# A two-layer transformer on one core: the image loads ahead of the weights, a bias folded into weights, powers apart, and a new stage order with three added matmuls

## The reference

```python
h = _L0_tok_ref(x, L0_tok_channel_weights)
h = jnp.concatenate([h, txt], axis=1)
h = h + _L0_attn_ref(_layernorm(h, axis=-1), ...)
h = h + _L0_ffn_ref(_layernorm(h, axis=-1), ...)
h = h + _L1_attn_ref(_layernorm(h, axis=-1), ...)
h = h + _L1_ffn_ref(_layernorm(h, axis=-1), ...)
```

## Time and profile before

| | us |
|---|---|
| median of 3 runs | 4835.94 (4804.51, 4835.94, 4847.9) |
| the profiled execution, whole | 4793.07 |
| its span, first to last instruction | 4791.3 |
| TensorE busy | 4135.2 (86% of the span) |
| VectorE, ScalarE, POOL busy | 2621.2, 1759.9, 402.3 |
| mean granted TensorE clock | 0.855 of 2.4 GHz |

### The profile page before, as it was taken

One profiled execution on the slowest core, in us unless ns is written; L12 is line 12 of the kernel. 1 busy time (PEld: TensorE's weight loads), 2 busy tenths in 40 slices (PEclk: granted clock), 3 DMA queues, 4 the chain that ended last, 5 costly groups with the idle time before them and its releaser, 6 DMA issues.

```text
span 4791.3 us, 70127 instructions
## 1 busy us (share of the span) xinstructions
PE 4135.2 (86%) x27744; PEld 3228.1 (67%) x27744; DVE 2621.2 (55%) x7217; ACT 1759.9 (37%) x2774; POOL 402.3 (8%) x523
## 2 busy tenths in 40 slices
PE   2779888889888989888889888989889888989888
PEld 1556677676676767677676667767667776766666
DVE  2455555555655555555555655555655555565433
ACT  1234333334333334333334333344433333433332
POOL 2100000000000000000000000000000000000000
PEclk8678888888889888888888888888888888888888
DMA  4111111101111101111101111101111110111000
GB/s 113 31 27 34 32 26 36 33 21 34 32 26 36 33 21 34 32 26 36 33 21 34 32 29 34 36 17 34 36 32 26 36 33 21 34 26 16 13 13 4
DMA packets 154046, 147.13 MB, mean 31 GB/s; under 512 B 64359, under 2 KB 132026, under 8 KB 153722
## 3 DMA queue, kind: packets, MB, share of 16 engines
q1 hardware_dynamic: 153722, 142.64, 14.0%
HBM read 87.28 MB, written 7.91 MB: 20 GB/s over the span
## 4 chain that ended last, share of the span: by engine, by line
PE 62%; DVE 19%; SPq 5%; ACT 5%; DMA 4%; issue 3%; POOL 3%; POOLq 0%; DVEq 0%; ACTq 0%
PE area_a L1034 13%; PE area_n L1042 11%; PE area_b L1034 8%; PE area_m L1042 7%; SPq L457 5%; PE area_n L1259 4%; DMA k1s<-scratch 3%; PE area_n L1066 3%; DVE mx L938 3%; PE area_m L1209 2%; ACT pT_both L666 2%; PE area_a L1117 2%; PE area_b L1057 2%; DVE scratch L949 1%; PE area_m L1066 1%
## 5 line engine op out<-in xcount | busy, mean ns | idle before, releaser
L938 DVE TENSOR_REDUCE mx<-area_n 91x1 f32<-91x273 f32 x1152 | 472.1, 432 | 246.5 <-PE area_n L1259 236.1
L1042 PE MATMUL area_n<-w_dn,hid 128*91 128x192 f32 x2304 | 494.8, 380 | 46.5 <-DVE mrow L943 38.7
L1034 PE MATMUL area_a<-xT,w_gu 96*128 96x273 f32 x1536 | 446.4, 438 | 61.7 <-DVE y L898 38.2
L1042 PEld LDWEIGHTS area_n<-w_dn,hid 128*91 128x91 f32 x2304 | 426.4, 190 | 95.3 <-issue 60.3
L1259 PE MATMUL area_n<-k1s,q1s 96*91 96x273 bf16 x1152 | 350.1, 359 | 152.5 <-DVE mx L938 92.9
L1034 PE MATMUL area_b<-xT,w_gu 96*128 96x273 f32 x1536 | 430.3, 426 | 0.0
L1034 PEld LDWEIGHTS area_a<-xT,w_gu 96*128 96x128 f32 x1536 | 305.0, 208 | 154.2 <-DVE y L898 48.0
L1259 PEld LDWEIGHTS area_n<-k1s,q1s 96*91 96x91 bf16 x1152 | 142.3, 141 | 335.3 <-DVE mx L938 227.2
L1034 PEld LDWEIGHTS area_b<-xT,w_gu 96*128 96x128 f32 x1536 | 313.0, 208 | 73.1
L611 ACT ACTIVATE pa<-area_a,scal 91x820 bf16<-91x820 f32 x192 | 180.3, 939 | 302.3 <-PE area_a L1117 278.2
L949 DVE RECIPROCAL scratch<-area_n 128x273 f32<-128x273 f32 x96 | 179.1, 1866 | 157.1 <-PE area_n L1280 157.1
(11 more groups left out here) (242 smaller groups left out, 7595.4 us busy)
## 6 DMA issues: line engine op xcount, KB each, us to landing
img<-in_x SPq DMA_DIRECT2D x192, 392.0 KB, 3.4
q1s<-scratch SPq DMA_DIRECT2D x192, 102.4 KB, 3.4
k1s<-scratch SPq DMA_DIRECT2D x192, 102.4 KB, 4.4
out<-outb SPq DMA_DIRECT2D x32, 204.8 KB
q0s<-scratch SPq DMA_DIRECT2D x128, 25.6 KB, 3.6
k0s<-scratch SPq DMA_DIRECT2D x128, 25.6 KB, 2.8
pooled<-pooled_dram SPq DMA_DIRECT2D x128, 9.2 KB
tokens<-in_txt SPq DMA_DIRECT2D x32, 57.8 KB
```

What stands on the lines that cost most here:

```text
L938: v.tensor_reduce(mx[:, k:k + 1], N[0:TC, k % 2, 0:T], AX.X, ALU.max)\
L1034: last = mm(area[x][0:rows_, j, 0:n], w(j, kc), rhs[:, kc, 0:n], start=(kc == 0), stop=(kc == NK - 1))
L1042: last = mm(by_token(x)[:, c, :], lhs(i, c), w_, start=(i == 0), stop=(i == len(w) - 1))
```

## The change

Five things:

1. *Start.* SP begins with the image. The constants that the first two turns need (38 copies) are started by ScalarE's queue; the 22 of layer 1 are started by SP at the beginning of turn 1 (`later_loads`) and awaited at turn 2. VectorE sums the first image before it waits for constants (`prepare()` in turn 0). ScalarE waits for the prepared weights at its first `a0`, TensorE at its first `pr0`.
2. *Bias row.* `r1` and hb1_ready go. proj_b is loaded into row 16 of w_p1, where the matching row of oN is the sum of weights divided by itself. `pr1` adds h1 directly.
3. *Deviations apart.* POOL raises each of the two inverse deviations by itself; the double one is first and has its own semaphore.
4. *Order.* `TURN` is new.
5. *Fill.* In front of `mx.1`, `mx.12` and `mx.17` TensorE does one matmul of weights on weights, whose result is overwritten.

```diff
-tok n4s n4n n4f cw n0s n1s n2n n0n qk1.0 qk1.1 v2 n0f qk0.0 pool.0 qk0.1 n2f ey.0 v1 ez.0 ey.1 mx.0 mx.1 mx.2 n1n gate
+n4s n4n tok n1s n0s cw n0n n2n n4f qk1.0 qk1.1 v2 ey.0 n0f r2 n2f ez.0 qk0.0 qk0.1 v1 pool.0 ey.1 ez.1 mx.0 mx.1 mx.2
...
+FILL = {"mx.1": 1, "mx.12": 1, "mx.17": 1}
...
+        load(w_p1[HD:HD + 1, 0, :], ins["L1_attn_proj_b"].rearrange("(a n) -> a n", a=1))
...
         def _(sp):
-            sp.wait_ge(zeroed, 4)
-            with nc.allow_non_contiguous_dma(reason="vectors onto partitions, once"):
-                for dst, src in loads:
-                    sp.dma_start(dst, src).then_inc(weights_in, 16)
             for k in range(NSLOT):
                 sp.dma_start(img[:, k, :], img_dram[0, :, k, :]).then_inc(image_in[k], 16)
 
             def program(t):
+                if t.it == 1:
+
+                    sp.wait_ge(zeroed, 4)
+                    with nc.allow_non_contiguous_dma(reason="vectors onto partitions, once"):
+                        for dst, src in later_loads:
+                            sp.dma_start(dst, src).then_inc(later_in, 16)
...
                     if twice:
-                        n = 2
-                        g.tensor_scalar(rstd[l][:, 1, :], var, 1.0 + EPS, EPS * EPS, ALU.mult, ALU.add)
+                        link(g.tensor_scalar(rstd[l][:, 1, :], var, 1.0 + EPS, EPS * EPS, ALU.mult, ALU.add))
+                        power(l, 1).then_inc(twice_ready, 1)
                     link(g.tensor_scalar(rstd[l][:, 0, :], var, EPS, None, ALU.add))
-                    r_ = rstd[l][:, 0:n, :].rearrange("p a c -> p (a c)")
-                    g.tensor_tensor(r_, r_, minus_half[0:TC, 0:n * NC_], ALU.pow).then_inc(rstd_ready[l], 1)
+                    power(l, 0).then_inc(rstd_ready[l], 1)
...
-                    elif stage == "r1":
-                        t.await_last("N", stage, "mx")
-                        if "dy.0" in t.stages:
-                            t.await_taken("N", "dy.0")
-                        add_row(hb1, h1, bproj1).then_inc(hb1_ready, 1)
...
         def _(act):
             a = nc.scalar
+            act.wait_ge(zeroed, 4)
+            with nc.allow_non_contiguous_dma(reason="vectors onto partitions, once"):
+                for dst, src in loads:
+                    act.dma_start(dst, src).then_inc(weights_in, 16)
...
+                if t.it == 2:
+                    pe.wait_ge(later_in, 16 * len(later_loads))
...
+                    for i in range(FILL[stage]):
+                        mm(area[x][:, bank, 0:D], w_dn[:, i % NEXP, 0, 0:128], w_dn[:, i % NEXP, 1, :], start=True, stop=True)
```

More of the change, by code:

```diff
@@ L64 @@
 OFFSET.update({x: 1 for x in ("r3 n1s n1n n2n n2f gate k1 v1 rta rtb pk0 gt pk1 s1 t1 c1 ct wo mg n3s n3n n3f f0 fd".split())})
-OFFSET.update({x: 2 for x in "n4s n4n n4f r1 qk1 v2 mx mt a2 pw os ob pr1 n5s n5n n5f rtr".split()})
+OFFSET.update({x: 2 for x in "n4s n4n n4f qk1 v2 mx mt a2 pw os ob pr1 n5s n5n n5f rtr".split()})
 OFFSET.update({x: 3 for x in "cw ey ez dy".split()})
@@ L151, in early_fusion @@
         w_p0 = sb("w_p0", [128, 3, NG, D], BF16)
-        rows = sb("rows", [TC, 6, D])
-        bproj0, bv0, bo, bf2, bv1, bproj1 = [rows[:, i, :] for i in range(6)]
+        rows = sb("rows", [TC, 5, D])
+        bproj0, bv0, bo, bf2, bv1 = [rows[:, i, :] for i in range(5)]
         norm_gb = sb("norm_gb", [KC, 4, NK])
@@ L526, in link, with power @@
                     pool.wait_ge(pool_step, base_step + steps[0])
+                def power(l, k):
+                    return g.tensor_tensor(rstd[l][:, k, :], rstd[l][:, k, :], minus_half[0:TC, 0:NC_], ALU.pow)
                 def inv_std(l, stage, of_turn, k, twice=False):
@@ L606, in program @@
                     elif name == "a0":
+                        if t.image(stage) == 0 and k == 0:
+                            act.wait_ge(weights_ready, 1)
                         for i, x in enumerate("AB"):
@@ L820, in program @@
                     elif name == "n2n":
-                        dve.wait_ge(rstd_ready["B"], n * 2 + 1)
+                        dve.wait_ge(twice_ready, t.done(stage))
                         normal("B", h0, xn2, 1).then_inc(xn_ready["B"], 1)
                     elif name == "n1n":
+                        dve.wait_ge(rstd_ready["B"], n * 2 + 1)
                         link(normal("B", h0, y))
@@ L953, in program @@
                         t.await_full("N", stage)
-                        dve.wait_ge(hb1_ready, t.done(stage))
-                        v.tensor_tensor(hb1[:, :, :], by_token("N"), hb1[:, :, :], ALU.add).then_inc(taken["N"], 1)
+                        v.tensor_tensor(hb1[:, :, :], by_token("N"), h1[:, :, :], ALU.add).then_inc(taken["N"], 1)
                     elif name == "n5s":
@@ L1068, in weigh, with fill @@
                     last.then_inc(full[x], 1)
+                def fill(stage, name, k):
+                    x, bank = areas(stage)[0], 0
+                    if name in ("pv", "mx"):
+                        bank = k % 2
+                        t.begin_bank(x, stage, name)
+                    elif name == "pw":
+                        t.begin_bank(x, stage, "ob")
+                    else:
+                        bank = int(name == "ob")
+                        t.begin(x, stage)
+                    for i in range(FILL[stage]):
+                        mm(area[x][:, bank, 0:D], w_dn[:, i % NEXP, 0, 0:128], w_dn[:, i % NEXP, 1, :], start=True, stop=True)
                 for stage in t.stages:
@@ L1074, in program @@
                     x = pair_of(name, k)
+                    if stage in FILL:
+                        fill(stage, name, k)
                     if name == "tok":
```

97 lines of the change are left out of this document (52 added, 45 removed).

## The result

| | before | after |
|---|---|---|
| median of 4 runs, us | 4827.33 (4804.51 to 4847.9) | 4661.63 (4641.93 to 4681.17) |
| the profiled execution, us | 4793.07 | 4641.93 |
| its span, us | 4791.3 | 4639.9 |
| mean granted clock, of 2.4 GHz | 0.855 | 0.878 |

The ratio is 0.965, with a 95% interval of 0.9613 to 0.9686: 3.5% faster. I had forecast 4718 and a range of 4600 to 4815.

The account below looks back on a forecast made before the run. TensorE's queue, its waits and its granted clock were taken to bound each turn. From the profiled 4793 us, -23 for the start and -1.8 a turn x 29 = -52 gave 4718, range 4600 to 4815.

Parts of the forecast that it names:

- The start: Program start and turn 1: 36 us gained by earlier statistics, 13 given back by the late text copy, -23 in all.
- Both marks of time: Signs at the start: first statistics near 36 us, and in turn 1 near 102.
- The fills: Three added matmuls among the row maxima: +0.5 us a turn for their cost, -2.1 through a higher clock.
- `r1` and its two waits go, hidden before: POOL's `r1` dropped with the bias row: costed at nothing, as already hidden.
- The powers apart: At a turn's start, separate powers let normalisation and pieces begin earlier: -0.4 us a turn, 1.1 lost to POOL's `r2` addition.
- The new order: Rearranged stages of a turn: small terms at `tok`, `ey.0` and from `mt` to `fd`, +0.2 us a turn together.
- +0.8 for `tok`: At a turn's start, pooled sums return later since `pool.5` follows `og.2`; mostly covered by `n4f`'s wait: +0.8 us (0 to +4).
- -0.9 from `mt` to `fd`: Stage from `mt` to `fd`: `ey.6` loses its 1.3 us wait, 0.7 returns at `n3f`, `mt` gains 0.3: -0.9 us a turn.
- the term of the maxima: Stage of the 36 row maxima: 51.3 to 49.2 us by a higher clock, -2.1 a turn, against +0.5 for added matmuls.
- rival B: The clock recovers by one step more: turns of 136.4 us, 4590 in all; chance 0.16.
- A: The fills don't lift the clock in the maxima: turns stay at 143.4 us, 4793 in all; chance 0.24.
- C: Slower: late image sums lengthen TensorE's pause before `tok` to 6 us, clock falls, turns 146.8, 4892 in all; chance 0.10.

Follow-up runs that it names:

- eleventh experiment: The second kernel with the old start, all constants on SP ahead of the image: median 4589.36 us, ratio 0.9516.
- second kernel: The changed kernel, fills kept, with the stage order of before (less `r1`): median 4574.56 us, ratio 0.9485.
- eighth experiment: The changed kernel with the image sums `pool.4` and `pool.5` moved earlier, behind `os.1` and `ez.7`: median 4722.06 us, ratio 0.9773.
- fourth: The changed kernel with `r2` late again, behind `mx.16`: median 4639.45 us, ratio 0.9614.
- tenth: The second kernel with `mt` ahead of `ct` and `ey.6`, `pw.2`, `ez.6` ahead of `mg`, as in the new order: median 4631.16 us, ratio 0.9575.

## Why the prediction was right, and where not

- **The start.** Forecast -23; 15 to 22 in the eleventh experiment, and 183.76 for the first `fd`, 22.0 earlier than before's 205.77. Both marks of time came out (36.65, 103.60). The constants landed 0.7 late, since the last copy's issue ended at 25.09 and not at 23.5: it took 2.99 us, where that of before took 0.26. From its end to the landing it was 5.3 us, and not 6.2. The sums' trip from the write to the first read took 9.0 (17.31 to 26.30) and not 4.8. The two queues shared what moves the bytes, as the Trainium skill (DMA: Bandwidth & Descriptors, "Issuing engines are not separate DMA queues") says. The trace agrees: the DMA share in these 9.0 us is 1.12, and 0.61 in the 4.8 of before. The longer trip stayed hidden, since the statistics also wait for VectorE's preparations. In the new order only 9 us of the start's 22 are left at the third `fd` (471.36, before 480.14); the turn behind the first `fd` has 149.9 us, where it has 135.4 in the second kernel. I had not foreseen it, and its cause was not looked for.
- **The fills.** -1.6 a turn forecast with their cost, -2.2 measured in the new order. Right in sign, a quarter short in size. Their price was short too: one fill takes 0.49 us, as in this row of the second kernel, and not the 0.35 that I took from the earlier trace rows.

```profile
2407.67 0.49 PE L1098 MATMUL area_n<-w_dn 128*128 128x192 f32 x2
```

- **"`r1` and its two waits go, hidden before", at nothing.** This step failed. The bias row with the end of `r1` is worth 98 us by itself. I had the row of a meeting of POOL and VectorE in hand and used it for the addition that was moved in; I did not look for the one that was taken out.
- **The powers apart, -0.4 a turn.** Undersized: 71 us by themselves, 2.4 a turn. I counted the VectorE time they save. What I left out is the wait for the keys that goes in 19 turns (26.8 us in all) and the clock behind `mx.0`, which is 0.79 in place of 0.77 and gives 1.5 us a turn.
- **The new order.** Its terms (+0.8 for `tok`, +0.3 for `ey.0`, -0.9 from `mt` to `fd`) came to +0.2 a turn, some 6 us. It costs 87. The waits came as described: 2.4 a turn at `tok` after the stage before (forecast 3.4 in all), `n4f` no longer held, 1.1 at `n3f` for 0.7. The stage from `mt` to `fd` came out exactly, 45.5 us for 46.4. What I missed is the new meeting of `r3` and `v0`, 1.2 a turn, that the maxima run at a low clock more often, and the 16 us before the third `fd`.
- **Why the sum held all the same.** The forecast was 75 less than the profiled time of before and the kernel gained 151. By stage the turn lost some 4.7 us where I had 1.8: 0.2 from `fd` to the first maximum (forecast +0.7), 0.9 from `mt` to `fd` (forecast -0.9) and 3.7 in the maxima (forecast -1.6). So the term of the maxima was sized at less than half of what it measured. Two edits booked at next to nothing brought more than the order, booked at next to nothing, gave back. That these two errors had opposite signs is luck. The range held since it reached toward rival B, whose 136.4 a turn was near the 137.9 that came; its reason ("the clock recovers by one step more") was right, its cause was not known to me.
- **Rivals.** A fell: fills do lift the clock (0.87 in the maxima, 0.79 without them). C fell at its own test: the wait is 2.4 in the mean where C wanted 6, and the eighth experiment, which takes it away, is slower.

The second kernel beats both: the same edits with the order of before, 4574.56 us, ratio 0.9485.

What stays open: how much of the order's 87 us is the meeting of `r3` (the fourth and eighth kernels move other pieces and don't give them back, and the tenth adds one to the old order and loses by it), how `r1` lowered the clock of the maxima, and why long turns hold at 143.4.

## What to carry to other kernels

When TensorE's clock varies, ask of each stage whether something else bounds it: a low clock there is free, and lifting it only lets TensorE arrive early and wait in front of the stage where the clock counts. Here the product of length and clock told that the kernels differ mostly by the clock of one stage. Before costing an edit at nothing, look at what each removed or moved POOL instruction meets on VectorE, as one does for added ones: the spread of an instruction's duration, minimum to maximum, shows it. And time an order change apart from the edits it comes with: here the other four parts were worth 5% and the order hid a third of it.
